# Cross-attention on one core: the weighing of the tile four back placed ahead of the new tile's scores in each turn of TensorE

## What is computed

```python
# x: (16, 100, 128) queries; ctx_1024: (16, 1444, 128) keys and values; 16 heads of 64
q = (pre_q @ Wq + bq).reshape(b, ql, H, D_Q)
k = (pre_k @ Wk + bk).reshape(b, kl, H, D_Q)
v = (pre_k @ Wv + bv).reshape(b, kl, H, D_Q)
scores = einsum('bqhd,bkhd->bhqk', q, k) / sqrt(D_Q)
attn = softmax(scores, axis=-1)
ctx = einsum('bhqk,bkhd->bqhd', attn, v).reshape(b, ql, H * D_Q)
x = pre_q + ctx @ Wo + bo
return (x - mean(x)) * rsqrt(var(x) + 1e-5) * gamma + beta
```

## Time and profile before

| | |
|---|---|
| median of three runs | 1032.2 us |
| the profiled execution: its own time | 1032.44 us |
| the profiled execution: span, first to last instruction | 1030.6 us |
| granted clock of TensorE, mean (1 is full speed) | 0.955 |
| TensorE busy | 914.7 us, 89% |
| VectorE busy | 825.5 us, 80% |
| ScalarE busy | 737.1 us, 72% |
| GpSimd busy | 288.5 us, 28% |
| transfers, share of 16 DMA engines | 89.8% |

### The profile page before, as it was taken

One profiled execution on the slowest core, in us unless ns is written; L12 is line 12 of the kernel. 1 busy time (PEld: TensorE's weight loads), 2 busy tenths in 40 slices (PEclk: granted clock), 3 DMA queues, 4 the chain that ended last, 5 costly groups with the idle time before them and its releaser, 6 DMA issues.

```text
span 1030.6 us, 25345 instructions
## 1 busy us (share of the span) xinstructions
PE 914.7 (89%) x10330; PEld 692.1 (67%) x10330; DVE 825.5 (80%) x1058; ACT 737.1 (72%) x1079; POOL 288.5 (28%) x342
## 2 busy tenths in 40 slices
PE   7699793998888889898999989998999989999897
PEld 6476572676666667676776757666777767677676
DVE  4797584776788868898889878888888878899784
ACT  3676575575777857786788868787687868788674
POOL 1141245331313323132332323232232313232001
PEclk8999897898999989999999999999999999999999
DMA  7488787788999989997989989999899989999897
GB/s 205 105 162 163 153 126 152 134 154 169 170 183 192 175 155 188 192 201 172 183 190 208 184 174 195 192 203 183 163 186 194 194 173 192 194 190 181 177 174 148
DMA packets 684879, 181.17 MB, mean 176 GB/s; under 512 B 655511, under 2 KB 683994, under 8 KB 684762
## 3 DMA queue, kind: packets, MB, share of 16 engines
q1 hardware_dynamic: 683418, 179.01, 89.8%
q10 hardware_dynamic: 1344, 0.53, 0.2%
HBM read 15.35 MB, written 0.82 MB: 16 GB/s over the span
## 4 chain that ended last, share of the span: by engine, by line
PE 52%; SPq 14%; DMA 13%; issue 9%; DVE 8%; POOL 3%; ACT 1%; POOLq 0%; DVEq 0%; ACTq 0%
PE ps L516 21%; PE ps L530 14%; PE ps L535 9%; DMA pt_lo<-p_lo 9%; SPq L330 6%; PE ps L403 5%; SPq L338 4%; DMA ct_lo<-c_lo 3%; DVE nmax L727 3%; DVE p_lo L742 3%; SPq L282 2%; PE ps L397 1%; SPq L311 1%; POOL rstd L953 1%; POOL early_sb L971 1%
## 5 line engine op out<-in xcount | busy, mean ns | idle before, releaser
L727 DVE TENSOR_REDUCE nmax<-ps 128x1 f32<-128x1446 f32 x200 | 332.2, 1661 | 106.1 <-PE ps L516 105.6
L742 DVE SCALAR_TENSOR_TENSOR p_lo<-p,rinv,p_hi 128x1444 f16<-128x1444 f32 x200 | 368.9, 1844 | 9.5 <-DMA pt_lo<-p_lo 6.5
L844 ACT ACTIVATE p<-ps,nmax 128x1446 f32<-128x1446 f32 x200 | 292.1, 1461 | 44.2 <-DVE nmax L727 43.8
L852 ACT ACTIVATE p_hi<-p,rinv 128x1444 f16<-128x1444 f32 x200 | 298.7, 1493 | 1.2 <-DMA pt_hi<-p_hi 1.2
L530 PE MATMUL ps<-pt_hi,c_hi 128*128 128x128 f16 (+1 forms) x2288 | 278.2, 221 | 4.7 <-ACT xT L620 3.5
L530 PE MATMUL ps<-pt_hi,c_lo 128*128 128x128 f16 (+1 forms) x2288 | 278.3, 221 | 0.0
L530 PEld LDWEIGHTS ps<-pt_hi,c_hi 128*128 128x128 f16 x2288 | 222.2, 100 | 32.8 <-issue 6.1
L530 PEld LDWEIGHTS ps<-pt_hi,c_lo 128*128 128x128 f16 x2288 | 221.9, 100 | 19.8 <-issue 0.5
L864 ACT ACTIVATE o_t<-ps,unscale 128x128 f32<-128x128 f32 (+1 forms) x208 | 74.4, 362 | 202.3 <-PE ps L535 202.2
L516 PE MATMUL ps<-ct_lo,g_hi 128*128 128x482 f16 (+3 forms) x624 | 163.9, 382 | 32.5 <-DMA ct_lo<-c_lo 32.5
L535 PE MATMUL ps<-pt_lo,c_hi 128*128 128x128 f16 (+1 forms) x2288 | 160.8, 220 | 30.0 <-DMA pt_lo<-p_lo 29.9
(11 more groups left out here) (99 smaller groups left out, 671.3 us busy)
## 6 DMA issues: line engine op xcount, KB each, us to landing
c_raw<-in_ctx_dram SPq DMA_DIRECT2D x32, 256.0 KB
pt_hi<-p_hi SPq DMA_TRANSPOSE x200, 3.4
pt_lo<-p_lo SPq DMA_TRANSPOSE x200, 3.5
c_raw<-in_ctx_dram SPq DMA_DIRECT2D x16, 192.0 KB
c_raw<-in_ctx_dram SPq DMA_DIRECT2D x48, 18.0 KB
out_dram<-y SPq DMA_DIRECT2D x16, 50.0 KB
x_sb<-in_x_dram SPq DMA_DIRECT2D x1, 600.0 KB
o_t<-in_L_xattn_Wq_dram SPq DMA_DIRECT2D x2, 256.0 KB, 4.4
```

Source lines behind the costliest of these rows:

```text
L727: dve.tensor_reduce(nmax[:, n % RING:n % RING + 1], ps[:, bank:bank + 3, 0:KEYW], AX.XY, ALU.max, negate=True).then_inc(s_nm, 1)
L742: dve.scalar_tensor_tensor(out=p_lo[:, par, 0:KL], in0=p32[:, n % P32S, 0:KL], scalar=rinv[:, i:i + 1], in1=p_hi[:, par, 0:KL], op0=ALU.mu ...
L844: act.activation(p32[:, n % P32S, :].rearrange("p (k w) -> p k w", w=KEYW), ps[:, bank:bank + 3, 0:KEYW], ACT.Exp, bias=nmax[:, i:i + 1], ...
L852: act.activation(p_hi[:, par, 0:KL], p32[:, n % P32S, 0:KL], ACT.Copy, scale=rinv[:, i:i + 1]).then_inc(s_hi, 1)
```

## The change

In the loop over the turns, the call of `weigh(n - LAG)` moves from behind `scores(n)` to ahead of it, together with the one wait that belongs to the first of them. Nothing is added or removed, and the other engines' programs stay as they are.

```diff
             for n in range(N + LAG):
+                if n == LAG:
+                    emptied(pe, J_X3 - 1)
+                if n >= LAG:
+                    weigh(n - LAG)
                 if n < N:
                     if n == 0:
                         for k in (J_G, J_G + 1):
@@
                             emptied(pe, k)
                     scores(n)
-                if n == LAG:
-                    emptied(pe, J_X3 - 1)
-                if n >= LAG:
-                    weigh(n - LAG)
                 if n < N:
                     job(n)
                 else:
```

## The result

The changed kernel takes 1162.07 us (median of four runs, 1159.67 to 1172.58), the kernel before 1034.69 us on the same chips (median of four, 1025.92 to 1037.46). The ratio is 1.1267, 95% interval 1.1167 to 1.1367: slower by 12.7%. The prediction of 1124 us had the direction. The time lies within its range of 8 in 10, 1058 to 1172, near the upper end, and above the range of 1085 to 1155 that it gave to its forecast alone. Of the 127 to 130 us that came on top it had 92.

What follows compares the result with a forecast made beforehand. TensorE's own work was taken to bound the kernel; 1032.4 us + 26.3 (loop) + 60 (disturbances) + 5 (first turns) gave 1124 us, own range 1085 to 1155, 8 in 10 range 1058 to 1172.

Steps and rivals of the forecast that it cites:

- The feedback loop: Scores, row maximum, lo part, its transpose, weighing, scores two tiles on: 9.90 us per two turns, 26.3 us more in all.
- Issue to the first matmul that uses it: Loop piece from issuing the lo transpose to the weighing's first matmul with pt_lo: 3.48 us.
- loads and context transposes: Transfers queued around lo transposes, delaying them: 2.4 us a batch for context loads, 1.0 for context transposes at r = 9 and 10.
- The wait for the context: TensorE at a batch's first tile waiting for ct_hi and ct_lo: 1.5 of the former 4.5 us a batch remain.
- the finished rows: At r = 10 they stand between row maximum and lo part: 2.56 in place of 1.84 us, 0.72 more.
- Sum of the steady part: The 170 turns from turn 29 on: 26.3 us more from the undisturbed loop plus 60 us from disturbances.
- the disturbances: Delays added to the loop without slack: 7.4 us a batch, share 0.6, 13.6 batches, 60 us more.
- The first 29 turns: Mostly held by GpSimd and the prologue; some ten run at TensorE's pace: 5 us more.
- The second loop: Through ScalarE's exponential and emptying of the bank, then a whole weighing: 9.1 us per two turns, hidden by 0.8 us.
- The clock at nothing: TensorE's waits of 0.3 to 1.2 us a turn were expected not to lower its clock: nothing in the sum.
- rival 3: The clock falls: three low-clock stretches a batch slow TensorE's scores, 45 us on top, 1169 us; chance 0.11.
- The chain: Chain of waits made of the loop's five pieces: pt_lo transfer about 35%, VectorE as much.

Runs made afterwards that it cites:

- experiment 1: Kernel before with order scores, job, weighing but the old distance (weighing of tile m ahead of scores of m+5): 1031.67 us, ratio 1.0035.
- experiment 2: Changed kernel with LAG = 3 in place of 4, the weighing one tile closer still: 2378.45 us (one run).
- experiment 3: One extra VectorE maximum per turn between row maximum and lo part: on the changed kernel 1209.82 us, on the kernel before 1036.32 us.
- experiment 6: Changed kernel loading only 16 of 128 partitions of each context third from the third batch on: 1152.25 us, ratio 1.1224.
- experiment 9: Changed kernel with hi transposes replaced by a small copy from the third tile on: 1085.72 us, ratio 1.0552.
- experiment 5: Transposes of the next context issued one turn earlier: on the kernel before 1000.83 us, on the changed kernel 1163.27 us.
- experiment 8: Changed kernel with ScalarE emptying the bank of the weighing one slot earlier: 1176.35 us, ratio 1.1452.

## Why the prediction was right, and where it fell short

**The feedback loop.** Right. Putting the weighing one tile closer made a loop over two turns. With the old distance the same order costs 0.35% (experiment 1), with one less the loop closes in one turn and is all there is (experiment 2), and 0.6 us on its VectorE piece costs 50 us (experiment 3). Its undisturbed length, predicted as 9.90 us, is 9.81 in the turns shown: 4.66 + 5.15. TensorE waits for `pt_lo` as forecast (120.4 us, 100 to 200 expected), SyncE no longer for the weighing, and the mean clock stayed at 0.956.

**Issue to the first matmul that uses it, 3.48 us.** This is the step that failed in size. I took two rows near the median, but a chain without slack adds up means. A quarter of the landings takes 5 us, in the kernel before as in the changed one, and its range to 5.9 stood in the earlier trace rows. Measured is 4.13 us; 0.65 / 2 x 170 = 55 us. Of the 4.13, 3.82 is the landing, where I had 3.44, and 0.31 the time from the landing to the matmul, where I had 0.04: 32 and 23 us. The second comes from 40 of the 168 turns, in which TensorE reached the lo part more than 0.15 us after the landing; in most of them it had been busy without a break, in three it had waited for the bank. It looks like one loop held up by the other on TensorE; no run separates that. I had put part of the first under loads and context transposes, together 3.4 of 7.4 us a batch. The loads were to cost 2.4 x 0.6 x 13.6 = 20 us; they are some 5 (experiment 6). What does it in the main is the hi transpose of every turn (experiment 9), which I had waved off as landing "well ahead": it does, but I had looked only at when it lands and not at what it does to the lo one.

**The wait for the context, 1.5 us a batch, and the finished rows.** I had the first at 1.5 x 0.6 x 13.6 = 12 us. The wait is gone nearly altogether (3.4 us in all), and to issue it earlier gives nothing (experiment 5). The 0.72 us at r = 10 is in the trace as predicted: 2.56 us from row maximum to lo part there, 1.84 elsewhere.

**Sum of the steady part.** Forecast 26.3 + 60 = 86 us, measured 112.4. By the table, the loop's mean is 0.99 us above my 9.90, 84 us; the disturbances I had at 60. That the whole still came into the range is partly luck. More than half of my 60, the loads and the wait for the context, was nearly not there, and the lateness of the lo transposes in every turn, which was, stood in no term. The upper end of the forecast's own range, 1155, doesn't follow from its terms either: with all of the 9 us a batch (122 us) they give 1032.4 + 26.3 + 122 + 5 = 1186.

**The first 29 turns, 5 us.** It was 17. No run looked into that stretch.

**The second loop, hidden by 0.8 us.** In time, yes: its waits appear (44.6 us, 65 times), but to remove them gained nothing (experiment 8).

**The clock at nothing.** The mean is unchanged, but in the kernel before most low stretches lay at the first tile of a batch, and now most follow a wait for the lo transpose, in the loop (same columns as above):

```profile
1034.00:1038.00 4.00, 1.59 (x14) 1.41 (x14) 1.54 (x1) 3.53 (x6) 0.44 (x1) 0.80 1.19 154
```

Here TensorE had waited 2.40 us, for a lo transpose issued at 1031.10. Filling the waits took two thirds of the low stretches away and some 6 us, within the uncertainty. The share of the clock in the loop can be read in part: of the 0.21 us by which the mean of the first piece is above 2.04 (18 us of time), half lies in the 16 turns whose scores ran partly at the low clock. I had held that only idle stretches of 3 us cost the clock, which the trace doesn't bear out; in the kernel before it already fell once behind a wait of 1.93 us, at 206.6 us. The measured 1162 is nearer to rival 3's 1169 than to my 1124, but not by its mechanism: rival 3 wanted three low stretches in each of 13.6 batches; there are 17 in all, and the low time from turn 29 on only went from 51.3 to 60.6 us. It happened in small.

**The chain.** I expected 35% transfers `pt_lo` and as much VectorE. They are 21% and 24%, and all transfers together 23%. The whole chain holds the first 29 turns too, and not every turn is held by that piece.

## What to carry to other kernels

When work is moved in a software pipeline, count by tiles, not by rows: "a few lines up" can mean one turn less between a result and the engine that made it. Add up the way from the consumer back to itself, divide by the turns that it spans, and compare with the busiest engine's turn; below it the loop is invisible, above it every piece of it costs, on engines that look idle. Sum such a loop with means and not medians, and look for what shares its queue.

## What I had not expected of the hardware

- Two transposes of some 128x1500 fp16 each turn, through one queue: the lo one takes 3.2 us from issue to landing when the hi ones are left out, but 4.9 to 5.0 us in the mean for 24 to 27% of them when hi and lo alternate (the hi one ahead issued 1.4 to 7 us before it, the next one 1.5 to 2.3 us behind it in the median).
- TensorE's clock fell during or behind single waits of 1.8 to 2.5 us, though not with all of them: 16 of the 29 of 1.8 us or more. With the waits for the bank gone, and about the same idle time in fewer and longer pieces, the low stretches grew from 60.6 to 94.0 us. That the longer pieces are the reason is likely, not shown.
